# A graph network's attention scores: float32r one-hots, scores in two halves, and split loads of the work table

## The reference

```python
h = (x @ W).reshape(N, HEADS, HEAD_DIM)            # 8 heads of 32
alpha_s = jnp.einsum('nhc,hc->nh', h, a_src)
alpha_d = jnp.einsum('nhc,hc->nh', h, a_dst)
e = alpha_s[src] + alpha_d[dst]
e = jnp.where(e > 0, e, NEG_SLOPE * e)             # 0.2
m = segment_max(e, dst); ex = jnp.exp(e - m[dst])
out = segment_sum(h[src] * (ex / denom[dst]), dst)
```

## Time and profile before

| | us |
|---|---|
| median of 3 runs | 8832.05 (8828.82 to 8837.01) |
| span of the profiled execution | 8830.1 |
| PE busy | 6600.0 |
| DVE busy | 5164.4 |
| POOL busy | 4060.3 |
| ACT busy | 2234.7 |

### The profile page before, as it was taken

The page is one execution under the profiler, slowest core; times in us unless marked ns, Lnnn a source line. Parts: engine busy times, 40 slices in busy tenths (PEclk is TensorE's granted clock), DMA queues, the critical chain, the costliest instruction groups (busy, mean ns, idle before and its releaser), DMA issues. The chain is left out here.

```text
span 8830.1 us, 116392 instructions
## 1 busy us (share of the span) xinstructions
PE 6600.0 (75%) x27378; PEld 5018.6 (57%) x27379; DVE 5164.4 (58%) x9644; ACT 2234.7 (25%) x4857; POOL 4060.3 (46%) x4373
## 2 busy tenths in 40 slices
PE   4977777774736666679999999974788885787886
PEld 2546566563525444546666666653676673666665
DVE  3138888886243333246666666665666666566666
ACT  1222222221310000123333333332333331333332
POOL 0025555552037777124444444423666661666663
PEclk9988888886857777589999999986777776677777
DMA  2247767666013333133343344332444441544443
GB/s 92 99 144 212 214 208 213 207 209 151 4 57 105 105 105 105 29 108 115 115 124 114 116 121 116 117 83 85 135 139 135 131 140 37 149 133 135 136 135 90
DMA packets 440058, 1096.42 MB, mean 124 GB/s; under 512 B 102452, under 2 KB 177296, under 8 KB 439410
## 3 DMA queue, kind: packets, MB, share of 16 engines
q0 software_dynamic: 249344, 763.23, 30.9%
q1 hardware_dynamic: 190180, 328.60, 11.1%
HBM read 1009.55 MB, written 81.94 MB: 124 GB/s over the span
## 5 line engine op out<-in xcount | busy, mean ns | idle before, releaser
L731 POOL DMA_INDIRECT st_rows<-g_table,st_stage_idx x1632 | 1558.0, 955 | 873.4 <-issue 463.6
L824 POOL DMA_INDIRECT st_rows<-kv_table,st_stage_idx x832 | 806.2, 969 | 671.1 <-PE st_psM L1167 391.2
L2385 PE MATMUL st_psM<-st_msg,st_hot 128*128 128x273 f32 x3264 | 942.6, 449 | 128.0 <-DVE st_msg L2233 102.6
L677 POOL DMA_INDIRECT st_rows<-p_table,st_stage_idx x816 | 854.3, 1047 | 302.9 <-issue 220.3
L731 POOL DMA_INDIRECT st_rows<-h_table,st_stage_idx x816 | 777.0, 952 | 244.5 <-issue 234.8
L2385 PEld LDWEIGHTS st_psM<-st_msg,st_hot 128*128 128x128 f32 x3264 | 702.9, 221 | 321.5 <-DVE st_msg L2233 91.2
L1519 DVE TENSOR_TENSOR st_pre<-st_psP,st_rows 128x512 f32<-128x512 f32 x816 | 523.5, 682 | 531.5 <-PE st_psP L1610 392.6
L1616 PE MATMUL st_psC<-st_w,st_rT 128*128 128x256 f32 x3264 | 814.7, 392 | 0.0
L1616 PEld LDWEIGHTS st_psC<-st_w,st_rT 128*128 128x128 f32 x3264 | 587.3, 190 | 373.7 <-ACT st_rT L1577 212.3
L1426 PE MATMUL st_psM<-st_rows,st_hot 128*128 128x256 f32 x1632 | 512.3, 484 | 372.5 <-DMA st_rows<-h_table,st_stage_idx 190.4
L1426 PEld LDWEIGHTS st_psM<-st_rows,st_hot 128*128 128x128 f32 x1632 | 401.3, 251 | 480.7 <-issue 331.3
(11 more groups left out here) (394 smaller groups left out, 11250.1 us busy)
## 6 DMA issues: line engine op xcount, KB each, us to landing
st_dst_row<-in_dst_row SPq DMA_DIRECT2D x310, 512.0 KB, 5.7
kv_table<-st_rows_out SPq DMA_DIRECT2D x25, 1560.0 KB, 5.7
st_ea<-in_ea SPq DMA_DIRECT2D x103, 256.0 KB, 3.8
st_rows<-g_table,st_stage_idx POOLq DMA_INDIRECT x1632, 2.8
st_pens<-pen_table SPq DMA_DIRECT2D x208, 72.0 KB
st_rows<-kv_table,st_stage_idx POOLq DMA_INDIRECT x832, 4.5
st_rows<-h_table,st_stage_idx POOLq DMA_INDIRECT x816, 2.7
st_rows<-p_table,st_stage_idx POOLq DMA_INDIRECT x816, 3.7
```

The lines of the kernel that those rows point to most:

```text
L677: pool.indirect_dma_start(out=rows[:, u * SLOTS + j, :], out_offset=None, in_=table, in_offset=bass.IndirectOffsetOnAxis(ap=stage_idx[:, u ...
L731: pool.indirect_dma_start(out=rows[:, slot, j, :], out_offset=None, in_=table, in_offset=bass.IndirectOffsetOnAxis(ap=stage_idx[:, g, u * ...
L824: pool.indirect_dma_start(out=rows[:, slot, j, :], out_offset=None, in_=kv_table, in_offset=bass.IndirectOffsetOnAxis(ap=stage_idx[:, g, u ...
L2385: last = nc.tensor.matmul(out[:, 0:MSG_W], onehots[:, j, :], msg[:, n, j, :], start=(j == 0), stop=(j == SLOTS - 1))
```

## The change

The GAT one-hots `hotrow` and `xhotrow` become float32r tiles. At the end of `gat_tables`, VectorE writes `dst_split`: the scores rounded to float32r, and beside them what the rounding left over. `bring` multiplies a one-hot with the 16 columns of both halves, and `edge_scores` adds first the one half and the rows, then the other half. The register loads of the work table are split in two: the counts `x0` and `x1` are loaded with a check of their bounds at run time, `b0` and `more` without one as before. This applies to every caller of `work_of` and `work_typed`.

```diff
     def work_of(eng, row):
+        _, counts = nc.values_load_multi_w_load_instructions(
+            work[0:1, ds(row, 1), 0:2].squeeze(1), engines=[eng.engine], min_val=0, max_val=NS * NB)
         _, values = nc.values_load_multi_w_load_instructions(
-            work[0:1, ds(row, 1), :].squeeze(1), engines=[eng.engine], min_val=0, max_val=NS * NB,
+            work[0:1, ds(row, 1), 2:4].squeeze(1), engines=[eng.engine], min_val=0, max_val=NS * NB,
             skip_runtime_bounds_check_because=BOUNDED)
-        return values
+        return (*counts, *values)
...
             def work_typed(eng, row):
+                _, counts = nc.values_load_multi_w_load_instructions(
+                    typed_work[0:1, ds(row, 1), 0:2].squeeze(1), engines=[eng.engine], min_val=0, max_val=NS * X_MAX)
                 _, values = nc.values_load_multi_w_load_instructions(
-                    typed_work[0:1, ds(row, 1), :].squeeze(1), engines=[eng.engine], min_val=0, max_val=max(n_nodes, NS * X_MAX),
+                    typed_work[0:1, ds(row, 1), 2:4].squeeze(1), engines=[eng.engine], min_val=0, max_val=max(n_nodes, NS * X_MAX),
                     skip_runtime_bounds_check_because=BOUNDED)
-                return values
+                return (*counts, *values)
...
+                    link.turn()
+                    link(v.tensor_copy(dst_split[:, :, 0, :], dst_alpha[:, :, :]))
+                    link(v.tensor_tensor(dst_split[:, :, 1, :], dst_alpha[:, :, :], dst_split[:, :, 0, :].bitcast(F32), ALU.subtract))
...
-            hotrow = st.sb("hotrow", [P, U, SLOTS, P])
-            xhotrow = st.sb("xhotrow", [P, SLOTS, P])
+            hotrow = st.sb("hotrow", [P, U, SLOTS, P], F32R)
+            xhotrow = st.sb("xhotrow", [P, SLOTS, P], F32R)
...
-                        link(v.tensor_tensor(et[:, :, :, :], group_view(psE),
+                        link(v.tensor_tensor(et[:, :, :, :], split_view(0),
                                              rows[:, U * g:U * g + U, :, D:GAT_W].rearrange("p u j h -> p j u h"), ALU.add))
+                        link(v.tensor_tensor(et[:, :, :, :], split_view(1), et[:, :, :, :], ALU.add))
...
-                                last = nc.tensor.matmul(group_view(psE)[:, j, u, :], onehots[:, j, :],
-                                                        dst_alpha[:, ds(b, 1), :].squeeze(1), start=(fresh and j == 0),
+                                at = (j * U + u) * 2 * H3
+                                last = nc.tensor.matmul(psE[:, at:at + 2 * H3], onehots[:, j, :],
+                                                        dst_split[:, ds(b, 1), :, :].rearrange("p b n h -> p (b n h)"), start=(fresh and j == 0),
                                                         stop=True, skip_group_check=True)
```

More of the change, by code:

```diff
@@ L20 @@
 F32 = mybir.dt.float32
+F32R = mybir.dt.float32r
 BF16 = mybir.dt.bfloat16
@@ L1977, in head_sums, with gat_tables @@
         return NODE[:, :, :].rearrange("p b (h c) -> p b h c", c=HW3)[:, :, :, 0:HW3 - 1]
-    def gat_tables(layer, dst_alpha, elu_source):
+    def gat_tables(layer, dst_alpha, dst_split, elu_source):
         with Stage(("h", "low", "low_exp", "elu", "hT_ps", "hT", "y", "rows", "alphas", "link_dve"), ("w_in", "r_out")) as st:
@@ L2062, in _, with gat_pass @@
                         last.then_inc(S["y"], 1)
-    def gat_pass(layer, dst_alpha):
+    def gat_pass(layer, dst_split):
         with Stage(("idx_staged", "scored", "hotrow", "expanded", "x_hotrow", "x_expanded", "to_scan_ps",
@@ L2105, in gat_pass, with split_view @@
             lanes = psX[0:LANES, :]
+            def split_view(n):
+                return psE[:, 0:SLOTS * U * 2 * H3].rearrange("p (j u n h) -> p j u n h", j=SLOTS, u=U, n=2)[:, :, :, n, :]
             def group_view(tile):
@@ L2493, in gnn @@
         dst_alpha = sb(top, "dst_alpha", [P, NB, H3])
+        dst_split = sb(top, "dst_split", [P, NB, 2, H3], F32R)
         weight = sb(middle, "weight", [P, NT + U * SLOTS])
@@ L2508, in gnn @@
         for layer in (1, 2):
-            gat_tables(layer, dst_alpha, layer == 2)
-            gat_pass(layer, dst_alpha)
+            gat_tables(layer, dst_alpha, dst_split, layer == 2)
+            gat_pass(layer, dst_split)
             group_passes[0] += 1
```

## The result

The changed kernel takes 9513.3 us (median of 4 runs, 9507.2 to 9518.6) where the kernel before took 8833.7 beside it: a ratio of 1.0771, 95% interval 1.0756 to 1.0786. It is 680 us slower; 147 us were predicted, and the range ended at 9085. The direction was right and most of the places were; the size was not.

The account below looks back on a forecast made before the run. DVE was taken to bound the typed pass, PE the edge MLP, POOL's gathers the weighted, no single engine the GAT passes. 493 d - 84 + 7 + 2 at d = 0.45 gives 147 us; 8832 + 147 = 8979 us, range 8850 to 9085.

Parts of the forecast that it names:

- What bounds each pass: Typed pass bound by DVE, edge MLP by PE, weighted by POOL's gathers; no engine above 1017 of 1287 us in GAT.
- PE's calls run under its matmuls: GAT passes: TensorE's work-table calls are covered by its matmuls and add nothing.
- the figure worked out for ScalarE alone: GAT passes: 96 of 146 exposed calls put on ScalarE; from this, 156 us expected for the other engines' reads.
- The price of a call, d: Every work-table call: the split, checked read costs 0.45 us more, ends 0.14 and 0.63, paid 493 times.
- the second load: Work-table call: splitting one four-word load into two two-word loads adds 0.24 us, between nothing and 0.344.
- One access rather than four: DVE's four-word loads: times close to 0.344 us read as a price per load, not per word.
- The two checks: Work-table call: checks and one more address priced as three register operations, 0.14 to 0.29 us, middle 0.21.
- the five exposed calls: Typed pass: five uncovered DVE calls a group in 51 groups, 255 d, 115 us.
- Rival B: Typed pass: DVE's longer loop fetches code anew, 17 turns of 3 us, 51 us more, 9030 us; chance 0.1.
- The expansion: GAT passes: one float32r load and matmul a slot cuts DVE's 133.0 us wait, saving 84 us.
- The added operation: GAT `edge_scores`: one more add, 0.39 us 68 times, 27 us, of which a quarter, 7 us, is counted.
- 493 d - 75: Whole kernel: net change from 493 exposed calls at d less 75 us for the other terms; 147 us at d = 0.45.

Follow-up runs that it names:

- e9: Against e1: VectorE alone reads the work tables with two two-word loads and two checks; the other engines use one four-word load. 9391.1 us.
- e10: Against e1: ScalarE, TensorE and SyncE read with two two-word loads and checks; VectorE keeps one four-word load. 8945.0 us.
- e11: e1 with VectorE keeping a group's counts in registers in the typed pass, two calls a group in place of four. 8753.5 us.
- e4: Changed kernel with its two two-word loads, but counts raised to at least zero by a register operation instead of checked. 9086.1 us.
- e3: Changed kernel with one four-word load in place of two two-word loads; both counts still checked. 9154.7 us.
- e1: Changed kernel with one four-word load and no checks, each count raised to at least zero; float32r expansion kept. 8794.1 us.
- e5: e1 with 84 never-executed instructions added to VectorE's typed loop, as long as in the changed kernel. 8893.1 us.
- e2: Kernel before, float32 expansion, with e1's read: one four-word load, counts raised to at least zero. 8850.0 us.
- e7: e1 with added loads of one to four words at several offsets on VectorE, ScalarE and TensorE after its last stage. One run 8840.3 us.

## Why the prediction was wrong, step by step

**What bounds each pass: right, but for TensorE in the GAT passes.** e9 and e10 show that in the typed and the edge MLP pass only VectorE's reads are paid, that the weighted pass pays nothing, and that the GAT passes pay on several engines. e11 got its 40 us from the same reading of exposed calls. That PE's calls run under its matmuls did not hold: TensorE's stand for "issue" ahead of `psE` grew from 34 to 250 us. No run shows what of it is paid, beside ScalarE's part, so that e10 came so close to the figure worked out for ScalarE alone may be luck.

**The price of a call, d: the step that failed.** It was put at 0.45 us, 0.14 to 0.63. For the second load I took 0.24, the argument being that at the dearest a half costs what the whole costs, 0.344. A half costs 0.53, so two cost 0.72 us more than one whole, twice that upper end (0.85 with what stands between them, by the edge MLP boundaries of e4). "One access rather than four", read from the closeness of the values in the earlier trace rows, fits the whole row, and just that doesn't carry over to a part of it. The two checks were put at 0.14 to 0.29 us together with an address, at the price of the register operations in the earlier trace rows. Those that form a check take 0.19 us each, not 0.045 to 0.097, and e3 has 0.58 us a call with the gaps. So d is 1.4 us where a call has both loads and 0.8 where it has the counts alone.

With it the terms come out thus. Typed pass: the five exposed calls cost 3.7 (three calls), 0.80 and 0.83 us a group, 5.3 us, 51 x 5.3 = 270 us instead of 115. Edge MLP pass: 147 instead of 41, for d and a little for the count, as 1.43 us are paid at 102 boundaries and not at the 92 at which PE waited before. GAT passes: 237 instead of 66 (the passes of the changed kernel less those of e1); how much of that is the price of a call, how much the calls that the prediction had as covered, and how much pauses at a loop's return, no run takes apart.

**Rival B came on top: 79 us.** It was right in kind: e5 shows that the longer body stands at its return. B had 17 turns of 3 us, 51 us, and a chance of 0.1; there are 16 returns of 4.9 us. The instructions that the change adds to a turn (18 calls with four more for their two checks, and 12 others, on 221) could have been counted beforehand and would have given it more weight, though no row told at which length a loop begins to stand.

**The expansion: right, a little too good.** Predicted 84 less 7, 77 us in the GAT passes; e2 less e1 has 65. The block was put at 0.6 us by the transposes of the earlier trace rows and takes 1.87 in the group shown, a little over the bound on the other side, 0.9 to 1.8: those transposes ran at a granted clock of 1.00 (the 2.4 GHz level), the block at 0.50. But the wait for `psE` fell by 106 us all the same. The rows gave 55 back, half, where 19 of 51 was the share taken. The added operation is hidden, nearly as said. (A slip in the sums: 493 d - 75 turns at d = 0.152, not 0.153, and is told from no change below 0.116, not 0.117; nothing hangs on it.)

The sum with the measured terms: 270 + 79 + 147 + 237 - 65 = 668 us, and 682 with the 14 us by which e2's GAT passes stand above those of the kernel before, against the 680 measured. Terms from single profiles are not exact to less than some 10 us.

## What to carry to other kernels

A register load, a bounds check or a register operation that sits ahead of a bound engine's next instruction is a cost of that engine, although no busy time shows it: count its calls on the path and take its price from a row of the very form that will run, since a smaller load need not be a cheaper one. Where a price has never been seen, its upper end is not that of the nearest larger thing. When instructions are added to a loop, count what they add to a turn, and look at the wait at the loop's return.

## What the runs showed of the hardware

A load of one, two or three words into registers takes 0.30, 0.52 and 0.75 us on VectorE, and of a whole row of four 0.345 (e7). A run-time check of one value takes two instructions, 0.19 and 0.023 us on VectorE, 0.15 and 0.018 on the others (the changed kernel). A longer loop can cost 5 us at each return without executing an instruction more (e5), and a loop that stands so can cease to when its code lies elsewhere (the weighted pass in e1 and e5). A float32r matmul leaves one record a slot where float32 leaves two, at about the same time a record (0.224 and 0.234 us at a granted clock of 0.50).
